# The prologue of a two-layer transformer kernel: when GpSimd splits a weight block, and in how many parts the modulation vectors are computed

## The chip, the cores and the metric

The kernel runs on one core of a Trainium2 chip. A core has five engines with instruction queues of their own, which meet only at semaphores: TensorE (PE, matmuls, with its weight loads shown as PEld), VectorE (DVE), ScalarE (ACT), GpSimd (POOL) and SyncE (SP, which here issues the DMAs). SBUF is the on-chip memory, PSUM the memory that TensorE writes. The metric is the time of one execution on the device in microseconds (us); the kernel before has a median of 677.3 us over three runs (677.08, 677.30 and 679.79).

## The reference

The input is x, 8 sequences of 256 tokens with 128 features. Two layers follow. Each has a modulation from a small conditioning input c: six vectors per layer, twelve in all, each for every sequence.

```python
mod = (_silu(L0_c) @ L0_wmod).reshape(8, 6, 1, -1)
sa, ca, ga, sb, cb, gb = (mod[:, i] for i in range(6))
ga = (2 * (ga >= 0) - 1) * jnp.maximum(jnp.abs(ga), 0.25)      # gb alike
h = _layernorm(x) * (1 + ca) + sa            # the first norm: needs sa and ca of layer 0 only
x = x + ga * attention(h)                    # 16 heads of 8, latent keys and values
h = _layernorm(x) * (1 + cb) + sb
x = x + gb * experts(h)                      # 8 experts, top 2, and a shared one
...                                          # layer 1, with its own six vectors:
x = x + ga * recurrent(_layernorm(x) * (1 + ca) + sa)   # gates, a scan over time, a gated MLP
x = x + gb * experts(_layernorm(x) * (1 + cb) + sb)     # 8 gated experts, top 2
```

In the attention, the latent is `gelu(h @ Wkd + bkd)`, its two halves added; keys and values come from it, and queries from h.

## The kernel before, in words

Tokens lie along the free dimension and features on the 128 partitions. The 2048 tokens are worked in four blocks of 512 (index t), a block being two sequences. The order on every engine is written out by hand in one function for each engine; what an engine may not start yet is held by a wait on a semaphore that stands in its queue, and everything behind that wait is held too.

The stages are: the prologue (loads, first norm, latent, values), the attention in 32 units (a sequence and a group of four heads each, n = 0 to 31), the first experts, the recurrent part of layer 1 with its MLP, and the second experts.

The prologue, engine by engine:

- **SP** loads the vectors, four blocks of x (L208), the modulation weights `WMOD` (L209, 768 KB), `KM`, and last the big block of matrices `M` (L211, 1384 KB), which holds also the recurrent layer's weights, 1664 columns of it.
- **TensorE** computes the means (L1140) of the four blocks, the variances of blocks 0 and 1 (L1153), then all twelve modulation vectors (L1190, 12 matmuls of 8 columns), then the variances of blocks 2 and 3, then the latent projection `kd` of the four blocks (L1199, waiting at L1198 for the two modulated sequences of its block). Then come the first unit's projections (L1207, L1208) and the values (L1314). A float32 matmul shows as two records in the profile.
- **ScalarE** squares (L386), takes logarithm and exponential of the variances (L392, L394), and later the four GELUs of the latent (L421), which wait for `kd`; a table load (L470) and the evacuation of unit 0 (L432 to L437) follow.
- **VectorE** centres (L645), waits for all twelve vectors, copies them out of PSUM (L767, L768), works out the gates (L771 to L779), and then normalises the four blocks: per block one multiplication by the reciprocal root (L652) and two `tensor_scalar` with the modulation (L656).
- **GpSimd** fills constants, flips signs in `KM` and `M` (L275 to L280), and then splits the recurrent layer's weights into an upper part `LH` (L282) and a rest `LL` (L284), each 128 x 1664. `LH` is also what TensorE's filler matmuls read (`keep_clock`, L1305). `LL` is first needed in layer 1, where TensorE waits for it at L1453. After the split GpSimd waits for the 32 `join` (L335), one for each attention unit.

In the attention, unit by unit, ScalarE evacuates a projection (L432 to L437), GpSimd joins it (L335), TensorE makes the scores (L1228, L1229), VectorE takes their maxima (L802) and spreads them into `MP` (`spread_max`: L813, then L815), TensorE transposes `MP` (`maxima_t`, L1282), VectorE adds it to the queries (L822), and TensorE makes the transposed scores (L1242 to L1246), whose exponentials ScalarE takes (L444); `values` (L1258, L1261), `spread_sum` (L828), `divide` (L836) and, once in four units, `place_values` (L843) complete it. GpSimd's own loop joins unit n + 3 at index n.

Of the kernel before, what the change touches and what calls it, by code (L numbers as in the profile page):

```python
# [5 lines left out]
BLK, NBLK = 512, 4  # L6
# [26 lines left out]
def build(nc, xT, wmod, vecs, mats, kmats, rows, b2, w0, w1, comb0, comb1, outT):  # L33
    f32, r32, bf16 = mybir.dt.float32, mybir.dt.float32r, mybir.dt.bfloat16
    ALU, ACT, AX = mybir.AluOpType, mybir.ActivationFunctionType, mybir.AxisListType
    ctx = ExitStack()
    with ctx:
        def sb(name, shape, dt=f32):
            return ctx.enter_context(nc.sbuf_tensor(name, shape, dt))

        def sem(name):
            return ctx.enter_context(nc.semaphore(name))

        def f(ap):
            return ap.bitcast(f32)

        def blk(tile, t, n=BLK):
            return tile[:, t * n:(t + 1) * n]
# [15 lines left out]
        LH = sb("LH", [128, MATS["l1"]], r32)  # L64
        LL = sb("LL", [128, MATS["l1"]], r32)
# [3 lines left out]
        MOD = sb("MOD", [128, 2, 6, 8])  # L69
        MC = sb("MC", [128, 2, 2, 8])  # L70
# [4 lines left out]
        SC = sb("SC", [128, 16])  # L75
# [7 lines left out]
        PS = ctx.enter_context(nc.psum_tensor("PS", [128, 8, 512], f32))  # L83
# [4 lines left out]
        def mat(name, i=0, n=128):  # L88
# [3 lines left out]
        WMOD = AR[:, 0:1536]  # L92
# [35 lines left out]
              for i, n in enumerate(("lg", "e", "k1", "k2", "e2", "w"))}  # L128
# [6 lines left out]
        const_done, ident_done, silu_done, mod_psum, mod_done, gate_done, sp_done = map(  # L135
            sem, ("const_done", "ident_done", "silu_done", "mod_psum", "mod_done", "gate_done", "sp_done"))
        mean_done, cen_done, sq_done, var_done, lnv_done, rstd_done, nrm_done, hn_done, hh_done, hl_done = map(
            sem, ("mean_done", "cen_done", "sq_done", "var_done", "lnv_done", "rstd_done", "nrm_done",
                  "hn_done", "hh_done", "hl_done"))
# [9 lines left out]
        l1_split = sem("l1_split")  # L149
        x_part = sem("x_part")  # L150
        qk_bias = sem("qk_bias")
        bias_done = sem("bias_done")
        flipped = sem("flipped")
        latent_one = sem("latent_one")
# [25 lines left out]
        def norm_at(k, t):  # L180

            return 8 + turns.index((k, t)) if k in (2, 3) else 4 * k + t
# [11 lines left out]
        def variance_bank(k, t):  # L194
            if k in (2, 3):
                return 4 + t
            return 6 + t % 2 if k == 4 else 4 + norm_at(k, t) % 2
# [51 lines left out]
        def _(gp):  # L249
# [29 lines left out]
            gp.tensor_scalar(qm[:, :, 0, :], qm[:, :, 0, :], -1.0, 0.0, ALU.mult, ALU.add).then_inc(flipped, 1)  # L279
            gp.tensor_scalar(qm[:, :, 2:4, :], qm[:, :, 2:4, :], -1.0, 0.0, ALU.mult, ALU.add).then_inc(flipped, 1)  # L280
            lm = M[:, MAT_AT["l1"]:MAT_AT["l1"] + MATS["l1"]]
            gp.tensor_scalar(LH[:, :], lm, 1.0, 0.0, ALU.mult, ALU.add).then_inc(l1_split, 1)  # L282
            gp.wait_ge(l1_split, 1)
            gp.tensor_tensor(out=LL[:, :], in0=lm, in1=f(LH[:, :]), op=ALU.subtract).then_inc(l1_split, 1)  # L284

            def split_weights(n, e, slot, width):

                s = moe[n]
                gp.tensor_scalar(WH[:, slot, 0:width], WS[:, 0:width], 1.0, 0.0, ALU.mult, ALU.add)\
                  .then_inc(s["split"], 1)  # L290
                gp.wait_ge(s["split"], 2 * e + 1)
                gp.tensor_tensor(out=WL[:, slot, 0:width], in0=WS[:, 0:width], in1=f(WH[:, slot, 0:width]),
                                 op=ALU.subtract).then_inc(s["split"], 1)
# [36 lines left out]
            def join(n):  # L330

                gp.wait_ge(qk_evac, 4 * n + 4)
                if n >= 4:
                    gp.wait_ge(st_done, 2 * n - 6)
                gp.tensor_tensor(out=QKX[:, n % 4, :, :], in0=QKT[:, :, :], in1=f(QKR), op=ALU.subtract)\  # L335
                  .then_inc(qx_ready, 2)
# [3 lines left out]
            for n in range(UNITS):  # L340
                if n + 3 < UNITS:
                    join(n + 3)
            gp.wait_ge(moe[0]["w_in"], 16)
            split_weights(0, 0, 0, 1024)
            for t in range(NBLK):
# [16 lines left out]
            for t in range(NBLK):  # L362
                for c in range(3):
                    i = 3 * t + c
# [277 lines left out]
        def _(dve):  # L642
# [2 lines left out]
                dve.tensor_tensor(out=blk(XC, t), in0=blk(X, t), in1=PS[:, mean_bank(k, t), :], op=ALU.subtract)\  # L645
                   .then_inc(cen_done, 1)

            def normalise(k, t):

                layer, which = k // 2 if k < 5 else 1, {0: 0, 1: 1, 2: 0, 5: 1}[k]  # L650
                dve.wait_ge(rstd_done, norm_at(k, t) + 1)
                dve.tensor_tensor(out=blk(HN, t), in0=blk(XC, t), in1=blk(STAT, t), op=ALU.mult)\  # L652
                   .then_inc(nrm_done, 1)
                dve.wait_ge(nrm_done, norm_at(k, t) + 1)
                for b in (2 * t, 2 * t + 1):
                    dve.tensor_scalar(blk(HN, b, SEQ), blk(HN, b, SEQ), MC[:, layer, which, b:b + 1],  # L656
                                      MOD[:, layer, 3 * which, b:b + 1], ALU.mult, ALU.add)\
                       .then_inc(hn_done, 1)

            def rms(k, src, weight, t):  # L660
                dve.wait_ge(rstd_done, norm_at(k, t) + 1)
                dve.scalar_tensor_tensor(out=blk(XC, t), in0=blk(src, t), scalar=vec(weight),
                                         in1=blk(STAT, t), op0=ALU.mult, op1=ALU.mult)\
                   .then_inc(nrm_done, 1)
# [97 lines left out]
                centre(0, t)  # L762


            dve.wait_ge(mod_psum, 1)
            mp = PS[:, 7, 0:96].rearrange("p (l i b) -> p l i b", l=2, i=6)
            dve.tensor_copy(MOD[:, :, :, :], mp).then_inc(mod_done, 1)  # L767
            dve.tensor_scalar(MC[:, :, :, :], mp[:, :, 1::3, :], 1.0, None, ALU.add).then_inc(mod_done, 1)  # L768
            dve.wait_ge(mod_done, 2)
            gates = MOD[:, :, 2::3, :]  # L770
            dve.tensor_scalar(GS[:, :, :, :], gates, 0.0, 2.0, ALU.is_ge, ALU.mult).then_inc(gate_done, 1)  # L771
            for layer in range(2):
                dve.scalar_tensor_tensor(out=GA[:, layer, :, :], in0=gates[:, layer, :, :], scalar=-1.0,
                                         in1=gates[:, layer, :, :], op0=ALU.mult, op1=ALU.max)\
# [5 lines left out]
                                     in0=GS[:, :, :, :].rearrange("p l w b -> p (l w b)"), scalar=-1.0,  # L780
                                     in1=GA[:, :, :, :].rearrange("p l w b -> p (l w b)"),
                                     op0=ALU.add, op1=ALU.mult).then_inc(gate_done, 1)
            for t in range(NBLK):
                normalise(0, t)
            def all_values(j):

                dve.wait_ge(v_psum, j + 1)
                dve.tensor_tensor(out=VALL[:, 4 * j:4 * j + 4, :],
                                  in0=PS[:, 2 + j, :].rearrange("p (i c) -> p i c", i=4),
                                  in1=ROWS[:, 0:128].unsqueeze(1).to_broadcast([128, 4, 128]), op=ALU.add)\  # L790
                   .then_inc(vall_done, 1)
# [113 lines left out]
            centre(1, 2)  # L905
            divide(31, 31, 0)
            normalise(1, 0)
            normalise(1, 1)
            attended(3)
            normalise(1, 2)  # L910
# [67 lines left out]
            for t in range(NBLK):  # L978
                i = projected.index((3, t))
# [3 lines left out]
                                         in1=blk(I_, t), op0=ALU.add, op1=ALU.mult).then_inc(hsi_done, 1)  # L983
# [140 lines left out]
        def _(pe):  # L1124
# [17 lines left out]
            def variance(k, t):  # L1142
                at = norm_at(k, t)
                pe.wait_ge(sq_done, at + 1)
                if k == 1 and t == 0:
                    pe.wait_ge(exp_done, 2 * UNITS)
                if k in (2, 3):
                    pe.wait_ge(cen_done, 8 + t + 1)
                    if k == 3:
                        pe.wait_ge(lnv_done, norm_at(2, t) + 1)  # L1150
                elif at >= 2:
                    pe.wait_ge(lnv_done, at - 1)
                pe.matmul(PS[:, variance_bank(k, t), :], OND[:, :], blk(STAT, t), start=True, stop=True)\  # L1153
                  .then_inc(var_done, 1)
# [30 lines left out]
            variance(0, 1)  # L1185
            pe.wait_ge(in_mod, 16)
            pe.wait_ge(silu_done, 1)
            for layer in range(2):
                for i in range(6):
                    mm = pe.matmul(PS[:, 7, 48 * layer + 8 * i:48 * layer + 8 * i + 8],  # L1190
                                   WMOD[:, 768 * layer + 128 * i:768 * layer + 128 * i + 128],
                                   SC[:, 8 * layer:8 * layer + 8], start=True, stop=True)
            mm.then_inc(mod_psum, 1)
            variance(0, 2)
            variance(0, 3)
            pe.wait_ge(in_mats, 16)
            for t in range(NBLK):
                pe.wait_ge(hn_done, 2 * t + 2)  # L1198
# [114 lines left out]
            for i in range(16):  # L1313
                mm = pe.matmul(PS[:, 2 + i // 4, 128 * (i % 4):128 * (i % 4) + 128],  # L1314
                               LAT[:, 128 * i:128 * i + 128], KM[:, 512:640], start=True, stop=True)
                if i % 4 == 3:
                    mm.then_inc(v_psum, 1)
            pe.wait_ge(ident_done, 9)
            pe.wait_ge(mod_done, 2)
            pe.wait_ge(l1_split, 1)  # L1320
            scores(0, 0, 0)
            project(1, 1, 0)
# [332 lines left out]
```

## Time and profile before

| | |
|---|---|
| median of three runs | 677.3 us |
| the profiled execution | 679.79 us, its span 678.0 us |
| PE, DVE, ACT, POOL busy | 606.8, 545.4, 486.1, 173.3 us |
| prologue, up to the end of the fourth `kd` matmul | about 29.1 us |
| one attention unit | about 4.4 us |

Times of the trace count from the start of the span; about 1.8 us of the execution lie outside it. "Busy" of PE counts a matmul from its start to a modelled end, so it says little about how full the array is. "PEclk" is the clock that TensorE was granted, 1.0 being 2.4 GHz and 0.50 being 1.2 GHz.

### The profile page before, as it was taken

What the parts mean: (1) busy time and instruction counts of PE and PEld (TensorE: products, weight loads), DVE (VectorE), ACT (ScalarE), POOL (GpSimd) and SP (SyncE); (2) the same over time, 40 slices, a digit from 0 to 9 for tenths busy, and PEclk for the clock granted to TensorE, in tenths of its full rate; (3) what the DMA queues carried; (4) which work ended last, traced back from release to release, by engine and by line L of the source; (5) the groups of instructions that cost most, each with busy time, mean ns of one, the idle gap of its engine ahead of it and who ended that gap; (6) DMA issues with size and microseconds to landing.
All of it is one profiled execution on the core that took longest, in us unless ns stands there. A gap on an engine that the chain in (4) does not pass through costs nothing.

```text
span 678.0 us, 11084 instructions
## 1 busy us (share of the span) xinstructions
PE 606.8 (89%) x3284; PEld 441.1 (65%) x3284; DVE 545.4 (80%) x1345; ACT 486.1 (72%) x857; POOL 173.3 (26%) x147
## 2 busy tenths in 40 slices
PE   8788889888997899999999999782699899999996
PEld 5355556555545568888888887351385788888884
DVE  3667888888866658878888887756899689999997
ACT  4548999999553669999999998677635466666663
POOL 3422223332301415443554443310143000000000
PEclk9789999999996899999999999976699799999999
DMA  7000000000100120122202220000000042222201
GB/s 239 1 0 2 2 2 0 0 0 0 32 1 0 48 113 37 57 95 94 91 2 93 93 85 1 23 1 0 0 1 0 1 150 87 87 86 86 86 1 62
DMA packets 6651, 29.85 MB, mean 44 GB/s; under 512 B 887, under 2 KB 1024, under 8 KB 4417
## 3 DMA queue, kind: packets, MB, share of 16 engines
q1 hardware_dynamic: 6610, 29.37, 12.2%
q8 instruction: 18, 0.29, 0.2%
q14 instruction: 23, 0.19, 0.1%
HBM read 28.18 MB, written 1.19 MB: 43 GB/s over the span
## 4 chain that ended last, share of the span: by engine, by line
PE 62%; DVE 26%; issue 5%; ACT 5%; DMA 1%; SPq 0%; POOL 0%; DVEq 0%; ACTq 0%; POOLq 0%
PE PS L1127 16%; PE PS L1129 16%; PE PS L1128 16%; DVE STAT L802 8%; PE PS L1273 2%; DVE RA L822 2%; PE PS L1228 2%; DVE HN L656 2%; PE PS L1153 2%; DMA AR<-in_wmod 1%; DVE SU L828 1%; PE PS L1242 1%; DVE HN L652 1%; ACT RA L605 1%; DVE AR L1086 1%
## 5 line engine op out<-in xcount | busy, mean ns | idle before, releaser
L937 DVE TENSOR_TENSOR RA<-AR,RA 128x512 fp32r<-128x512 f32 x140 | 134.3, 983 | 29.1 <-ACT RA L509 28.4
L508 ACT ACTIVATE AR<-PS,BI 128x512 f32<-128x512 f32 x144 | 99.4, 691 | 26.2 <-PE PS L1129 16.6
L1127 PE MATMUL PS<-HH,WH 128*128 128x512 f32 x272 | 109.5, 403 | 0.1
L1129 PE MATMUL PS<-HL,WH 128*128 128x512 f32 x272 | 107.4, 395 | 0.0
L1128 PE MATMUL PS<-HH,WL 128*128 128x512 f32 x272 | 107.3, 395 | 0.0
L509 ACT ACTIVATE RA<-PS,BI 128x512 fp32r<-128x512 f32 x144 | 98.4, 683 | 0.0
L802 DVE CUSTOM_DVE_ANT_0 STAT<-PS,MQ 128x128 f32<-128x128 f32 (+1 forms) x256 | 76.3, 354 | 20.2 <-PE PS L1229 20.1
L1127 PE MATMUL PS<-RA,WH 128*128 128x512 f32 x208 | 82.4, 396 | 2.5 <-DVE RA L1093 2.1
L1129 PE MATMUL PS<-RA,WH 128*128 128x512 f32 x208 | 81.2, 391 | 0.0
L1128 PE MATMUL PS<-RA,WL 128*128 128x512 f32 x208 | 81.2, 390 | 0.0
L312 POOL TENSOR_TENSOR AR<-AR 128x512 f32<-128x512 f32 x32 | 51.2, 1601 | 111.9 <-DVE AR L756 111.9
L335 POOL TENSOR_TENSOR RA<-QKT,RA 128x512 fp32r<-128x512 f32 x32 | 40.8, 1275 | 110.5 <-ACT RA L437 107.5
L605 ACT ACTIVATE RA<-AR 128x512 fp32r<-128x512 f32 x64 | 40.4, 632 | 34.2 <-DVE AR L1086 33.3
L1127 PEld LDWEIGHTS PS<-HH,WH 128*128 128x128 f32 x272 | 52.2, 192 | 15.6 <-ACT RA L509 3.0
L1129 PEld LDWEIGHTS PS<-HL,WH 128*128 128x128 f32 x272 | 51.9, 191 | 11.1
L1128 PEld LDWEIGHTS PS<-HH,WL 128*128 128x128 f32 x272 | 52.2, 192 | 10.7 <-issue 0.2
L444 ACT ACTIVATE AR<-PS 128x768 f32<-128x768 f32 x64 | 48.4, 808 | 13.7 <-PE PS L1246 11.6
L1153 PE MATMUL PS<-STAT,OND 128*128 128x512 f32 x48 | 31.5, 762 | 22.6 <-ACT STAT L386 22.6
L1093 DVE TENSOR_TENSOR RA<-AR,RA 128x512 fp32r<-128x512 f32 x64 | 44.3, 691 | 7.5 <-ACT RA L605 2.7
L599 ACT ACTIVATE AR<-PS 128x512 f32<-128x512 f32 x64 | 38.2, 597 | 13.8 <-PE PS L1129 11.8
L1127 PEld LDWEIGHTS PS<-RA,WH 128*128 128x128 f32 x208 | 39.2, 188 | 12.5 <-DVE RA L1093 3.2
L1086 DVE TENSOR_TENSOR AR<-AR 128x512 f32<-128x512 f32 x64 | 43.8, 685 | 2.2 <-ACT AR L614 2.2
(196 smaller groups left out, 1185.1 us busy)
## 6 DMA issues: line engine op xcount, KB each, us to landing
AR<-comb SPq DMA_DIRECT2D x16, 1024.0 KB, 4.6
WS<-in_w SPq DMA_DIRECT2D x9, 512.0 KB, 5.6
WS<-in_w SPq DMA_DIRECT2D x8, 384.0 KB, 3.1
M<-in_mats SPq DMA_DIRECT2D x1, 1384.0 KB, 12.2
X<-in_xT SPq DMA_DIRECT2D x4, 256.0 KB, 4.8
out_xT<-X SPq DMA_DIRECT2D x4, 256.0 KB, 2.1
AR<-in_wmod SPq DMA_DIRECT2D x1, 768.0 KB, 9.2
KM<-in_kmats SPq DMA_DIRECT2D x1, 162.5 KB
```

The costliest lines, as they stand in the source:

```text
L312: gp.tensor_tensor(out=blk(ACC, t), in0=blk(ACC, t), in1=YW[:, t % 2, :], op=ALU.add)\
L444: act.activation(PR[:, n0 % 2, 2 * h:2 * h + 2, :], PS[:, 2 + 2 * h:4 + 2 * h, 0:384], ACT.Exp, scale=SCALE).then_inc(exp_done, 1)
L508: act.activation(G[:, c, :], PS[:, c, :], ACT.Gelu_apprx_tanh, bias=bias).then_inc(s["act"], 1)
L509: act.activation(GH[:, m0 % 2, c, :], PS[:, c, :], ACT.Gelu_apprx_tanh, bias=bias)\
L605: act.activation(GH[:, m % 2, c, :], G[:, c, :], ACT.Copy).then_inc(s1["gh"], 1)
L802: mm = dve.tensor_tensor_reduce(out=MASKED_S[:, q, j, 0:width], in0=PS[:, j, first:first + width], in1=MQ[:, 256 - width:256], scale=-1.0, ...
L937: dve.tensor_tensor(out=GL[:, m0 % 2, c, :], in0=G[:, c, :], in1=f(GH[:, m0 % 2, c, :]), op=ALU.subtract).then_inc(s["lo"], 1)
L1086: dve.tensor_tensor(out=G[:, c, :], in0=G[:, c, :], in1=WB[:, e % 2, t * BLK:(t + 1) * BLK], op=ALU.mult).then_inc(s1["ymul"], 1)
L1127: pe.matmul(out, wh, xh, start=first, stop=False)
L1128: pe.matmul(out, wl, xh, start=False, stop=False)
L1129: return pe.matmul(out, wh, xl, start=False, stop=last)
L1153: pe.matmul(PS[:, variance_bank(k, t), :], OND[:, :], blk(STAT, t), start=True, stop=True)\
```

## The change

There are two edits.

The first is on GpSimd. `LH` is now made only once all eight sequences of the first norm are modulated (`hn_done` at 8), and `LL` not directly behind it but in the loop over attention units, at loop index 4, behind the join of unit 7.

The second is on TensorE and VectorE. The two vectors of the first norm are computed by two matmuls of their own (into PSUM bank 6), placed behind the variance of block 1. The twelve matmuls stay as they were but stand now behind the variances of blocks 2 and 3, ahead of `kd`. VectorE multiplies block 0 by its reciprocal root before it waits for the two vectors, copies only those, modulates, and copies the other ten and works out the gates after all four blocks.

```diff
@@ GpSimd
             lm = M[:, MAT_AT["l1"]:MAT_AT["l1"] + MATS["l1"]]
+            gp.wait_ge(hn_done, 8)
             gp.tensor_scalar(LH[:, :], lm, 1.0, 0.0, ALU.mult, ALU.add).then_inc(l1_split, 1)
-            gp.wait_ge(l1_split, 1)
-            gp.tensor_tensor(out=LL[:, :], in0=lm, in1=f(LH[:, :]), op=ALU.subtract).then_inc(l1_split, 1)
...
             for n in range(UNITS):
                 if n + 3 < UNITS:
                     join(n + 3)
+                if n == 4:
+                    gp.wait_ge(l1_split, 1)
+                    gp.tensor_tensor(out=LL[:, :], in0=lm, in1=f(LH[:, :]), op=ALU.subtract).then_inc(l1_split, 1)
@@ VectorE
+            divide_by_root(0, 0)
+            dve.wait_ge(mod_first, 1)
+            fp = PS[:, 6, 0:16].rearrange("p (i b) -> p i b", i=2)
+            dve.tensor_copy(MOD[:, 0, 0:2, :], fp).then_inc(mod_done, 1)
+            dve.tensor_scalar(MC[:, 0, 0, :], fp[:, 1, :], 1.0, None, ALU.add).then_inc(mod_done, 1)
+            dve.wait_ge(mod_done, 2)
+            modulate(0, 0)
+            for t in range(1, NBLK):
+                normalise(0, t)
             dve.wait_ge(mod_psum, 1)
...
-            dve.tensor_copy(MOD[:, :, :, :], mp).then_inc(mod_done, 1)
-            dve.tensor_scalar(MC[:, :, :, :], mp[:, :, 1::3, :], 1.0, None, ALU.add).then_inc(mod_done, 1)
-            dve.wait_ge(mod_done, 2)
+            dve.tensor_copy(MOD[:, 0, 2:6, :], mp[:, 0, 2:6, :]).then_inc(mod_done, 1)
+            dve.tensor_copy(MOD[:, 1, :, :], mp[:, 1, :, :]).then_inc(mod_done, 1)
+            dve.tensor_scalar(MC[:, 0, 1, :], mp[:, 0, 4, :], 1.0, None, ALU.add).then_inc(mod_done, 1)
+            dve.tensor_scalar(MC[:, 1, :, :], mp[:, 1, 1::3, :], 1.0, None, ALU.add).then_inc(mod_done, 1)
+            dve.wait_ge(mod_done, 6)
...
-            for t in range(NBLK):
-                normalise(0, t)
@@ TensorE
             variance(0, 1)
             pe.wait_ge(in_mod, 16)
             pe.wait_ge(silu_done, 1)
+            for i in range(2):
+                mm = pe.matmul(PS[:, 6, 8 * i:8 * i + 8], WMOD[:, 128 * i:128 * i + 128], SC[:, 0:8], start=True, stop=True)
+            mm.then_inc(mod_first, 1)
+            variance(0, 2)
+            variance(0, 3)
             for layer in range(2):
                 for i in range(6):
...
             mm.then_inc(mod_psum, 1)
-            variance(0, 2)
-            variance(0, 3)
             pe.wait_ge(in_mats, 16)
...
-            pe.wait_ge(mod_done, 2)
+            pe.wait_ge(mod_done, 6)
```

GpSimd's queue before, from the sign flips in `KM` and `M` on (`RA<-QKT,RA` is the join):

```order
L275 TENSOR_SCALAR KM<-KM 65x16x16
L276 TENSOR_SCALAR KM<-KM 65x16x8
L279 TENSOR_SCALAR M<-M 128x16x8
L280 TENSOR_SCALAR M<-M 128x16x16
L282 TENSOR_SCALAR LH<-M 128x1664
L284 TENSOR_TENSOR LL<-M,LH 128x1664
L335 TENSOR_TENSOR RA<-QKT,RA 128x512 x32
```

The same stretch of GpSimd's queue now:

```order
L276 TENSOR_SCALAR KM<-KM 65x16x16
L277 TENSOR_SCALAR KM<-KM 65x16x8
L280 TENSOR_SCALAR M<-M 128x16x8
L281 TENSOR_SCALAR M<-M 128x16x16
L284 TENSOR_SCALAR LH<-M 128x1664
L335 TENSOR_TENSOR RA<-QKT,RA 128x512 x8
L345 TENSOR_TENSOR LL<-M,LH 128x1664
L335 TENSOR_TENSOR RA<-QKT,RA 128x512 x24
```

The rest `LL` stands now between the eighth and the ninth join.

VectorE's queue before, from the centring on (`HN<-XC,STAT` is the multiplication by the root, `HN<-HN,MC,MOD` the modulation):

```order
L645 TENSOR_TENSOR XC<-X,PS 128x512 x4
L767 COPY MOD<-PS 128x96
L768 TENSOR_SCALAR MC<-PS 128x32
L771 TENSOR_SCALAR GS<-MOD 128x32
L773 SCALAR_TENSOR_TENSOR GA<-MOD 128x16 x2
L777 TENSOR_SCALAR GA<-GA 128x32
L779 SCALAR_TENSOR_TENSOR MG<-GS,GA 128x32
L652 TENSOR_TENSOR HN<-XC,STAT 128x512
L656 TENSOR_SCALAR HN<-HN,MC,MOD 128x256 x2
```

VectorE's queue now, from the same place:

```order
L648 TENSOR_TENSOR XC<-X,PS 128x512 x4
L654 TENSOR_TENSOR HN<-XC,STAT 128x512
L778 COPY MOD<-PS 128x16
L779 TENSOR_SCALAR MC<-PS 128x8
L662 TENSOR_SCALAR HN<-HN,MC,MOD 128x256 x2
```

The gates and the copies of the other ten vectors have moved behind the fourth block.

TensorE's queue before, from the means to the first unit's query projection (`PS<-SC,AR` are the modulation vectors, `64x512` is `kd`):

```order
L1140 MATMUL PS<-X,OND 128x512 x4
L1153 MATMUL PS<-STAT,OND 128x512 x2
L1190 MATMUL PS<-SC,AR 128x8 x12
L1153 MATMUL PS<-STAT,OND 128x512 x2
L1199 MATMUL PS<-HN,M 64x512 x4
L1207 MATMUL PS<-HN,M 128x256
```

TensorE's queue now, over the same stretch:

```order
L1159 MATMUL PS<-X,OND 128x512 x4
L1172 MATMUL PS<-STAT,OND 128x512 x2
L1208 MATMUL PS<-SC,AR 128x8 x2
L1172 MATMUL PS<-STAT,OND 128x512 x2
L1214 MATMUL PS<-SC,AR 128x8 x12
L1221 MATMUL PS<-HN,M 64x512 x4
L1229 MATMUL PS<-HN,M 128x256
```

The twelve small matmuls have changed places with the last two variances, and two more stand where the twelve stood.

## Rows read from the trace of the kernel before

**Rows 1.** The page: the chain that ended last, share of the span by engine.
```profile
PE 62%; DVE 26%; issue 5%; ACT 5%; DMA 1%; SPq 0%; POOL 0%; DVEq 0%; ACTq 0%; POOLq 0%
```

**Rows 2.** The chain in order of time, prologue: start, duration (us), what.
```profile
3.08 9.20 DMA AR<-in_wmod
...
12.32 2.86 PE PS L1190 x24
```

**Rows 3.** VectorE's instructions in order: start, duration (us), what, idle before.
```profile
16.30 0.69 DVE L652 TENSOR_TENSOR HN<-XC,STAT 128x512 f32<-128x512 f32 x1
17.02 2.22 DVE L656 TENSOR_SCALAR HN<-HN,MC,MOD 128x256 f32<-128x256 f32 x2
...
19.87 3.98 DVE L656 TENSOR_SCALAR HN<-HN,MC,MOD 128x256 f32<-128x256 f32 x2
...
24.50 0.73 DVE L656 TENSOR_SCALAR HN<-HN,MC,MOD 128x256 f32<-128x256 f32 x2
```

**Rows 4.** GpSimd's instructions in order, prologue.
```profile
17.48 1.61 POOL L282 TENSOR_SCALAR LH<-M 128x1664 fp32r<-128x1664 f32 x1
19.18 4.21 POOL L284 TENSOR_TENSOR LL<-M,LH 128x1664 fp32r<-128x1664 f32 x1
```

**Rows 5.** TensorE's instructions in order, prologue (two records to a matmul).
```profile
10.23 1.88 PE L1153 MATMUL PS<-STAT,OND 128*128 128x512 f32 x4
...
15.02 3.62 PE L1153 MATMUL PS<-STAT,OND 128*128 128x512 f32 x4
...
23.91 5.22 PE L1199 MATMUL PS<-HN,M 128*64 128x512 f32 x6 [3.48 <-DVE HN L656]
```

**Rows 6.** ScalarE's instructions in order, prologue.
```profile
12.01 0.63 ACT L394 ACTIVATE STAT<-STAT 128x512 f32<-128x512 f32 x1
...
14.30 0.61 ACT L386 ACTIVATE STAT<-XC 128x512 f32<-128x512 f32 x1
...
29.17 0.68 ACT L421 ACTIVATE AR<-PS,V 64x512 f32<-64x512 f32 x1 [0.86 <-PE PS L1199]
```

**Rows 7.** Windows: length, busy of PE, PEld, DVE, ACT, POOL, PEclk, DMA share, GB/s.
```profile
15.00:18.60 3.60, 3.60 (x6) 1.04 (x5) 3.25 (x10) 1.32 (x2) 2.25 (x3) 0.53 0.14 56
18.70:20.60 1.90, 1.04 (x2) 0.19 (x2) 1.86 (x3) 1.80 (x5) 1.82 (x2) 1.00 0.00 0
24.00:28.80 4.80, 4.80 (x6) 1.01 (x6) 3.02 (x10) 1.37 (x2) 0.00 (x0) 0.50 0.00 0
```

**Rows 8.** Weight loads of line 1153: duration in ns, least, median, most.
```profile
L1153 PEld LDWEIGHTS PS<-STAT,OND x8: 190/191/333, 9.8 to 16.7; 128*128 128x128 f32 x8
```

**Rows 9.** Lines 813 and 802: duration in ns, least, median, most.
```profile
L813 DVE CAST MP<-NM x32: 174/176/1042, 37.9 to 183.6; 128x8 fp32r<-128x8 f32 x32
...
L802 DVE CUSTOM_DVE_ANT_0 STAT<-PS,MQ x256: 282/356/425, 34.8 to 183.1; 128x128 f32<-128x128 f32 x64, 128x256 f32<-128x256 f32 x64
```

**Rows 10.** Units 0 and 6: GpSimd, VectorE and TensorE in order.
```profile
37.60 1.27 POOL L335 TENSOR_TENSOR RA<-QKT,RA 128x512 fp32r<-128x512 f32 x1 [3.45 <-ACT RA L437]
37.86 1.04 DVE L813 CAST MP<-NM 128x8 fp32r<-128x8 f32 x1
...
66.72 1.27 POOL L335 TENSOR_TENSOR RA<-QKT,RA 128x512 fp32r<-128x512 f32 x1 [3.21 <-ACT RA L437]
68.85 0.18 DVE L813 CAST MP<-NM 128x8 fp32r<-128x8 f32 x1
69.06 0.17 DVE L815 TENSOR_TENSOR MP<-NM,MP 128x8 f32<-128x8 f32 x1
69.34 0.38 PE L1282 MATMUL PS<-IDF,MP 128*128 128x128 f32 x2
...
71.33 1.27 POOL L335 TENSOR_TENSOR RA<-QKT,RA 128x512 fp32r<-128x512 f32 x1 [3.34 <-ACT RA L437]
```

**Rows 11.** TensorE by form, 39.0 to 42.4 us, then 42.5 to 46 us: busy us, mean ns.
```profile
L1228 PE MATMUL PS<-RA 32*128 32x128 f32 x2 | 0.5, 471 | 0.0
...
L1228 PE MATMUL PS<-RA 32*128 32x128 f32 x2 | 0.3, 322 | 0.1
```

More of the change, by code:

```diff
@@ L151, in build @@
         qk_bias = sem("qk_bias")
+        mod_first = sem("mod_first")
         bias_done = sem("bias_done")
@@ L646, in centre, with divide_by_root @@
                    .then_inc(cen_done, 1)
-            def normalise(k, t):
-                layer, which = k // 2 if k < 5 else 1, {0: 0, 1: 1, 2: 0, 5: 1}[k]
+            def divide_by_root(k, t):
                 dve.wait_ge(rstd_done, norm_at(k, t) + 1)
@@ L653, in normalise, with modulate @@
                    .then_inc(nrm_done, 1)
+            def modulate(k, t):
+                layer, which = k // 2 if k < 5 else 1, {0: 0, 1: 1, 2: 0, 5: 1}[k]
                 dve.wait_ge(nrm_done, norm_at(k, t) + 1)
@@ L658, in normalise @@
                        .then_inc(hn_done, 1)
+            def normalise(k, t):
+                divide_by_root(k, t)
+                modulate(k, t)
             def rms(k, src, weight, t):
```

## The prediction

> **What bounds the kernel now.** I read the page first: the chain that ended last is 62% TensorE and 26% VectorE, with 1% DMA and next to no GpSimd [rows 1]. GpSimd itself is thus not the bound. It can only matter by whom it holds up. The chain in order of time then shows who is late in the prologue: the modulation weights land 12.28 us into the span (3.08 + 9.20), the twelve small matmuls take 2.86 us behind them [rows 2], and only then does VectorE copy, work out the gates, and reach its first multiplication by the root at 16.30 [rows 3]. VectorE's instructions in order show the second thing. The two `tensor_scalar` of a block take 0.73 us where nothing disturbs them, but 2.22 us in block 0 and 3.98 us in block 1 [rows 3]. GpSimd's splits lie exactly there: `LH` from 17.48 to 19.09, `LL` from 19.18 to 23.39 [rows 4]. The excess is (2.22 - 0.73) + (3.98 - 0.73) = 4.74 us, and TensorE waits for it: 3.48 us of idle time before `kd` of block 1, which starts at 23.91 [rows 5]. The fourth `kd` ends near 29.13 (23.91 + 5.22), the last GELU starts at 29.17 [rows 5, 6], and all of unit 0 hangs on that one. So what the prologue gains is read at one point, the end of the fourth `kd`.
>
> The windows tell of TensorE's clock: it was granted 0.53 of full speed from 15.0 to 18.6, behind the twelve 8-column matmuls, 1.00 from 18.7 to 20.6, and 0.50 (1.2 GHz) from 24.0 to 28.8, behind a gap with one matmul in it [rows 7]. At 2.4 GHz two variances take 1.88 us, at the low clock 3.62, and three `kd` take 5.22 [rows 5]; so one such matmul is 0.94 us or 1.74 to 1.81 us.
>
> **The prologue after the change, step by step.** ScalarE has the root of block 0 at 12.64 (12.01 + 0.63) [rows 6]; VectorE multiplies until 13.3 (0.69 us) [rows 3]. The two first vectors are 4 of 24 records, 2.86 x 4/24 = 0.48 us, so they are there at 12.8 [rows 2]. Two small copies of about 0.2 us each and a pair of 0.73 us follow: block 0 is modulated at about 14.5. A square takes 0.61 us; that of block 2 stands right behind the root of block 0 and ends near 13.2, that of block 3 ended at 14.91 and can't come earlier [rows 6]. So TensorE, no longer held by twelve matmuls, does variance 2 at 13.2 and variance 3 from 14.93. Blocks 1 to 3 are then modulated at about 16, 18 and 19.6, at 0.69 + 0.73 us a block, with `LH` and `LL` out of the way. None of that is late, because TensorE has something else to do first: the twelve small matmuls now stand between variance 3 and `kd`. They were under the wait for the roots before; now they are on the path.
>
> - With the full clock throughout: 14.93 + 0.94 + 2.86 + 4 x 0.94 = 22.5. Gain 29.1 - 22.5 = 6.6 us.
> - With the low clock throughout: a weight load takes 0.33 us instead of 0.19 [rows 8], so the twelve take 2.86 x 0.33/0.19 = 5.0, and the sum is 14.93 + 1.81 + 5.0 + 4 x 1.74 = 28.7. Gain 0.4 us.
>
> What the clock does in between I can't know: small matmuls were followed by the low level before [rows 7], and two variances now lie among them. I take the middle, 3.5 us, and keep 0.4 and 6.6 as ends. The table load, the evacuation of unit 0, its join and its scores follow the last GELU as before and shift with it. The sign flips of `M`, as long as before, meet the modulation of block 2; TensorE's twelve matmuls hide that. `LH`, from about 19.6 to 21.3, is first needed at the scores of unit 0, behind the last `kd`, the GELU, a table load and the evacuation; it would have to be some 5 us late to be seen. The gates and the two additional copies, some 1.6 us on VectorE, fall in the same hole, even behind `LH`. SP issues nothing else, and no DMA is moved.
>
> **`LL` behind the join of unit 7.** GpSimd does nothing but one join of 1.27 us in each unit, and waits for 3.2 us in between [rows 10], so a piece of 4.21 us looks nearly free there. The join of unit 7 is the eighth, 66.72 to 67.99; `LL` would run from 68.09 to 72.30 by the times of before. Behind it in GpSimd's queue is the join of unit 8, which began at 71.33 [rows 10]. It would be 1 us late and end at 73.6; its first user, the scores of unit 8, stands behind a transposition one unit after the one at 69.34, so at 73.7 at the earliest: hidden. But VectorE has L813 at 68.85, a copy of 128 x 8 from SBUF to SBUF. It takes 176 ns in the median and once took 1042 [rows 9]. That once is unit 0: it started at 37.86 while GpSimd's join ran from 37.60 to 38.87, and it ended at 38.90, 0.03 us behind the join [rows 10]. So this copy waits for GpSimd's instruction to end, however small it is itself. Started at 68.85 under `LL`, it would end at 72.33 and not at 69.03: 3.3 us. Behind it in VectorE's queue are L815, the division, the sums' spreading, and the addition of the maxima; waiting for L815 is the transposition on TensorE, which started at 69.34 with 0.1 us to spare [rows 10]. The loss on the path is 3.2 us, and an attention unit has no slack that gives it back, as PE and DVE release each other in turn along the chain [rows 1]. Bounds: nothing, if the copy gets through, to 3.3.
>
> The Trainium skill, "SBUF — State Buffer", section "Who interferes with whom", speaks against the change at just this point: a copy in a mode that uses two ports and a GpSimd instruction exclude each other for a whole instruction, and whichever issues first goes first. The rows agree, 1042 ns under a join and 3.98 us under `LL`. If the two shared the port in proportion, as its page says they don't, the copy would lose a few tenths and the sum below would be 674.3.
>
> In these 3.2 us TensorE has nothing to do, and the last gap like it, 3.48 us, was followed by the low clock [rows 5, 7]. No row shows a whole unit at that clock; the nearest, the first scores' matmuls, take 471 ns instead of 322 [rows 11]. The low stretch between 15.0 and 18.6 lasted 3.4 us, from (1 - 0.53)/0.5 x 3.6 [rows 7]. 3.4 us of attention at that pace lose 3.4 x (1 - 322/471) = 1.1 us; two such stretches 2.2; none 0. It happens or not, so I take half of 1.1, that is 0.5.
>
> **The sum.** -3.5 + 3.2 + 0.5 = +0.2 us. On the profiled execution, 679.8 us with 678.0 us of span, that is 680.0. The profiled one was the slowest of the three; the median is 677.3, and the forecast for the median is 677.5 us. A difference of less than 0.5% (3.4 us) can't be told from no change in this kernel.
>
> **Rivals.**
>
> - *VectorE isn't held by `LL`.* Then only the prologue counts: 677.3 - 3.5 = 673.8, between 670.7 and 676.9 by the clock. For it: L802, which runs in every unit and beside the joins too, never took more than 425 ns, and only one L813 of 32 was ever long [rows 9]. Against it: that one waited to the end. 0.10.
> - *The clock holds through the prologue.* The two variances among the small matmuls keep TensorE at 2.4 GHz: -6.6 + 3.2 = 673.9. For it: after the first variances the clock was full. Against it: a single `kd` of 1.04 us ahead of a gap didn't hold it before [rows 7], and two with a dozen small ones might not either. 0.10.
> - *Slower: the low clock takes the prologue's gain and comes back in the attention.* The twelve small matmuls run at the low clock in front of `kd`, the fourth `kd` ends at 28.7, and the gap of 3.2 us in unit 6 is followed by one or two low stretches: -0.4 + 3.2 + 1.1 to 2.2 = +3.9 to +5.0, so 681.2 to 682.3. It decides once `kd` ends later than about 28. For it: three of four `kd` ran at 0.50 before [rows 7]. Against it: two variances in a row were followed by 1.00 at 18.7, and now TensorE's queue has no gap behind 15 us. 0.13.
> - *The two edits are too small to be seen for other reasons*, with some other wait of the same size ahead of unit 0: 677.3, 0.05.
>
> The forecast has 0.62. All of it, with its gain between 1.5 and 5.5 us, lies within 3.4 us of before, which gives 675.0 to 680.1 and counts as the same. Of the first two rivals about half passes the bound of faster (673.9): 0.11. Of the slower one nearly all passes 680.7: 0.12. Left for the same: 0.77. The range reaches from the middle of the first two rivals to the edge of the slower one, 673.9 to 681.0.
>
> **What would show it.** In the changed profile: all `tensor_scalar` of the modulation near 0.41 us each; the first multiplication at 12.7; the twelve small matmuls without a gap between variance 3 and the first `kd`; the last `kd` between 22.5 and 28.7, with PEclk saying why. In the attention: `LL` of 4.2 us behind the eighth join, one L813 (now with another line number) of 3.3 to 3.5 us under it, an idle TensorE ahead of one transposition, and perhaps a PEclk of 0.50 behind that. The prediction is wrong if that one copy is short, if something but `kd` sets the start of unit 0, or if the time moves by more than 3.4 us.

## The result, and the profile after

The changed kernel takes 736.17 us in the median of four executions (732.80 to 737.93), the kernel before 678.08 us (677.08 to 679.79). The ratio is 1.085, with a 95% interval of 1.081 to 1.088. I had forecast 677.5 us, 673.9 to 681.0, and the chance I gave to slower was 0.12.

The page of the changed kernel, part 2 (40 equal slices) and the chain's shares:

```profile
PE   8997999999999978999999999977369899999996
...
PEclk8798555555556968999999999998769889999999
...
PE 78%; DVE 13%; ACT 5%; issue 3%; DMA 1%; POOL 0%; SPq 0%; DVEq 0%; ACTq 0%; POOLq 0%
```

Eight slices in a row, of 18.3 us each, have a granted clock of about half (1.2 GHz). Before, the chain was 62% TensorE and 26% VectorE [rows 1]; now it is 78% and 13%. Something has made TensorE the bound of a whole stage.

First the prologue. TensorE's instructions in order, changed kernel (start, duration, what):

```profile
11.23 0.61 PE L1208 MATMUL PS<-SC,AR 128*128 128x8 f32 x4
12.28 1.13 PE L1172 MATMUL PS<-STAT,OND 128*128 128x512 f32 x2 [0.44 <-ACT STAT L389]
14.04 1.90 PE L1172 MATMUL PS<-STAT,OND 128*128 128x512 f32 x2 [0.63 <-ACT STAT L389]
15.73 5.13 PE L1214 MATMUL PS<-SC,AR 128*128 128x8 f32 x24
20.79 5.47 PE L1221 MATMUL PS<-HN,M 128*64 128x512 f32 x8
```

and two windows within `kd` (length, busy of PE, PEld, DVE, ACT, POOL, PEclk, DMA share, GB/s):

```profile
23.00:24.00 1.00, 1.00 (x2) 0.23 (x1) 0.00 (x0) 0.48 (x1) 0.00 (x0) 0.50 0.00 0
...
25.00:26.30 1.30, 1.30 (x4) 0.25 (x3) 0.00 (x0) 0.87 (x2) 0.00 (x0) 1.00 0.00 0
```

The fourth `kd` ends at 26.26 instead of 29.13 [rows 5]: 2.9 us earlier, where I had taken 3.5 between 0.4 and 6.6. About 0.9 us of that is not the change's: the blocks of x landed earlier in this execution, and the first variance began at 9.30, not 10.23. Counted from there the gain is 1.9 us. The twelve small matmuls run at the low clock (5.13 us, I had worked out 5.0), and `kd` stays at it until about 24.5 (the window from 24 to 25 us has 0.75); only its end is back at the high one. VectorE's modulation of a block takes 0.73 to 0.95 us, not 2.22 and 3.98 [rows 3].

Then unit 6 of the attention. GpSimd's instructions in order, then VectorE's, then TensorE's:

```profile
64.36 1.27 POOL L335 TENSOR_TENSOR RA<-QKT,RA 128x512 fp32r<-128x512 f32 x1 [3.21 <-issue]
65.59 3.70 POOL L345 TENSOR_TENSOR LL<-M,LH 128x1664 fp32r<-128x1664 f32 x1
69.25 1.26 POOL L335 TENSOR_TENSOR RA<-QKT,RA 128x512 fp32r<-128x512 f32 x1
```

```profile
66.48 2.84 DVE L832 CAST MP<-NM 128x8 fp32r<-128x8 f32 x1
69.36 1.18 DVE L834 TENSOR_TENSOR MP<-NM,MP 128x8 f32<-128x8 f32 x1
```

```profile
70.60 0.69 PE L1304 MATMUL PS<-IDF,MP 128*128 128x128 f32 x2 [3.46 <-DVE MP L834]
...
77.38 0.64 PE L1304 MATMUL PS<-IDF,MP 128*128 128x128 f32 x2
...
84.11 0.63 PE L1304 MATMUL PS<-IDF,MP 128*128 128x128 f32 x2
```

The stall is the one forecast, with one piece more: behind the copy, the subtraction of 128 x 8 (L834) also waits, until the join that follows `LL` is over at 70.51. Together they are about 3.7 us late, and TensorE is idle for 3.46 us. But then look at the distance of the transpositions, one to a unit: 6.78 and 6.73 us, where it was 4.39, from the 69.34 of [rows 10] to

```profile
73.73 0.39 PE L1282 MATMUL PS<-IDF,MP 128*128 128x128 f32 x2
```

The longer distance stays. Windows of the changed kernel (as above):

```profile
66.00:68.00 2.00, 1.14 (x6) 0.68 (x4) 1.97 (x5) 1.86 (x4) 2.00 (x1) 1.00 0.03 8
68.00:70.00 2.00, 0.00 (x0) 0.00 (x0) 1.97 (x2) 0.83 (x3) 2.00 (x2) 0.72 0.00 0
...
100.00:130.00 30.00, 30.00 (x194) 18.25 (x187) 17.86 (x105) 18.83 (x40) 5.96 (x5) 0.50 0.00 1
...
230.00:232.00 2.00, 2.00 (x6) 1.00 (x5) 1.97 (x3) 1.09 (x2) 2.00 (x1) 0.50 0.00 0
232.00:234.00 2.00, 2.00 (x5) 0.91 (x4) 0.95 (x5) 0.83 (x2) 0.02 (x1) 0.82 0.39 96
```

The clock falls to 1.2 GHz while TensorE waits, at about 68.9, and comes back at about 232.7 us, some 2.3 us into the first output projection, the first row of 128 x 512 matmuls since the stall:

```profile
230.39 4.76 PE L1295 MATMUL PS<-AR,M 128*128 128x512 f32 x8
```

For some 161 us of that TensorE is busy without a gap, and is the bound. At the low clock its attention matmuls are longer. One form, from 100 to 130 us, in the changed kernel (busy us, mean ns):

```profile
L1250 PE MATMUL PS<-RA 32*128 32x128 f32 x18 | 4.3, 472 | 0.0
```

and the same form in the same window of the kernel before:

```profile
L1228 PE MATMUL PS<-RA 32*128 32x128 f32 x28 | 4.6, 322 | 1.3 <-DVE NM L802 1.3
```

The account closes. The transposition of unit 6 is 1.26 us later than before (70.60 less 69.34: the stall of 3.6 less the 2.4 us by which its join was earlier, 64.36 for 66.72 [rows 10]). The last one, changed and before:

```profile
241.95 0.27 PE L1304 MATMUL PS<-IDF,MP 128*128 128x128 f32 x1
```

```profile
185.69 0.38 PE L1282 MATMUL PS<-IDF,MP 128*128 128x128 f32 x2
```

It is 56.3 us later. The span has grown by 733.7 - 678.0 = 55.7. So 55.0 us (56.3 - 1.3) lie between unit 6 and the last unit.

### The profile page after: what moved, and what is told of

Same layout as the page of the kernel before. It is cut to its first block, busy times and chain, and to the rows that moved or that the text cites. A ratio compares the mean times of both kernels' runs of the same rounds, so it can differ in the third digit from the quotient of the medians.

```text
span 733.7 us, 11097 instructions
## 1 busy us (share of the span) xinstructions
PE 676.5 (92%) x3288; PEld 479.8 (65%) x3288; DVE 548.8 (75%) x1349; ACT 490.6 (67%) x857; POOL 172.7 (24%) x147
## 2 busy tenths in 40 slices
DMA packets 6651, 29.85 MB, mean 41 GB/s; under 512 B 887, under 2 KB 1024, under 8 KB 4417
## 4 chain that ended last, share of the span: by engine, by line
PE 78%; DVE 13%; ACT 5%; issue 3%; DMA 1%; POOL 0%; SPq 0%; DVEq 0%; ACTq 0%; POOLq 0%
PE PS L1146 15%; PE PS L1148 15%; PE PS L1147 15%; PE PS L1268 4%; PE PS L1280 3%; PE PS L1250 3%; PE PS L1229 3%; PE PS L1230 3%; PE PS L1264 3%; PE PS L1295 2%; PE PS L1172 2%; PE PS L1304 2%; PE PS L1251 1%; PE PS L1283 1%; DVE STAT L821 1%
## 5 line engine op out<-in xcount | busy, mean ns | idle before, releaser
L447 ACT ACTIVATE AR<-PS 128x768 f32<-128x768 f32 x64 | 51.0, 810 | 37.6 <-PE PS L1268 37.6
L1095 DVE TENSOR_TENSOR AR<-PS,AR 128x512 f32<-128x512 f32 x64 | 43.9, 685 | 2.1 <-ACT AR L602 2.1
```

The source lines that it names most:

```text
L447: act.activation(PR[:, n0 % 2, 2 * h:2 * h + 2, :], PS[:, 2 + 2 * h:4 + 2 * h, 0:384], ACT.Exp, scale=SCALE).then_inc(exp_done, 1)
L1095: dve.tensor_tensor(out=G[:, c, :], in0=PS[:, 2 + c, :], in1=SG[:, c, :], op=ALU.mult)\
```

## The experiments

Theory A was: the stall lets the clock fall, and the attention's matmuls, which had kept the full clock before, don't bring it back. Against it stood B (the prologue's new order is to blame), C (`LL`'s place slows the attention by itself, by the port or by a shifted order), and later D (a gap is not enough, it takes GpSimd).

**`LL` in the prologue.**

```diff
             gp.wait_ge(hn_done, 8)
             gp.tensor_scalar(LH[:, :], lm, 1.0, 0.0, ALU.mult, ALU.add).then_inc(l1_split, 1)
+            gp.wait_ge(l1_split, 1)
+            gp.tensor_tensor(out=LL[:, :], in0=lm, in1=f(LH[:, :]), op=ALU.subtract).then_inc(l1_split, 1)
...
-                if n == 4:
-                    ...
```

> The changed kernel, with LL split directly behind the late LH, in the prologue, and no longer in the attention. Theory A (VectorE's copy is held by LL, TensorE stands still for 3.5 us, its clock falls to 1.2 GHz and the attention's matmuls never bring it back): no gap, so the clock stays at 1.00 through the attention and the time is before less the prologue's gain of 2.9 us, 675. Rival B (the new order of the prologue leaves the clock or the pipeline in a worse state for the attention): still about 730. Rival C (LL's place in the attention slows it by the shared port or by a shifted order, whatever the clock): 675 too.

676.39 us, ratio 0.998 (0.995 to 1.000). PEclk is 1.00 from 60 to 150 us. B falls: the prologue's order is that of the changed kernel.

**Only `LL` moved**, all else as before: the `LL` lines taken out of the prologue and put behind the join at loop index 4.

> The kernel before, with only LL moved behind the join of unit 7; LH and the whole prologue as before. Theory A: the gap and the low clock from unit 6 on, 678 + 4 + 25 units x 2.3 us = about 738. Rival B: only the stall, 682. Rival C: about 738.

733.62 us in two executions, ratio 1.083. The move of this one instruction costs 55.7 us of the 58.1 that both edits together cost. In its windows:

```profile
66.00:70.00 4.00, 0.94 (x6) 0.61 (x6) 3.88 (x6) 1.56 (x5) 2.97 (x2) 0.69 0.00 0
70.00:100.00 30.00, 30.00 (x198) 17.73 (x196) 17.62 (x102) 18.14 (x39) 5.10 (x4) 0.50 0.00 1
100.00:220.00 120.00, 120.00 (x751) 72.87 (x751) 70.70 (x402) 77.01 (x162) 22.52 (x18) 0.50 0.00 0
```

**The gap filled.** The changed kernel, `LL` where it is, and in unit 6 ahead of the transposition 14 fillers, matmuls of 128 x 512 whose results nobody reads (the diff is cut: TensorE's units 4 to 27 are also written out instead of looped):

```diff
+                if it == 0 and n0 == 5:
+                    pe.wait_ge(qm_ready, n + 1)
+                    pe.wait_ge(ot_done, n - 1)
+                    for _ in range(14):
+                        pe.matmul(PS[:, 7, :], LH[:, 0:128], LH[:, 0:512], start=True, stop=True)
...
```

> The changed kernel with LL where it is, but 14 filler matmuls (128 x 512, results unused) on TensorE ahead of the one transposition that waits for VectorE, so that TensorE has no gap. TensorE's step function for units 4 to 27 is written out instead of looped. Theory A: VectorE is still held for about 4 us, but the clock stays at 1.00: 678 - 2.9 + 4 = 679. Rivals B and C: still about 736.

679.95 us, ratio 1.004 (1.001 to 1.006). VectorE is held as long as before, TensorE has next to no gap. VectorE's instructions in order, TensorE's, then a window:

```profile
65.70 2.90 DVE L832 CAST MP<-NM 128x8 fp32r<-128x8 f32 x1
68.63 1.21 DVE L834 TENSOR_TENSOR MP<-NM,MP 128x8 f32<-128x8 f32 x1
```

```profile
66.02 3.54 PE L1321 MATMUL PS<-LH 128*128 128x512 f32 x14
69.90 0.44 PE L1304 MATMUL PS<-IDF,MP 128*128 128x128 f32 x2 [0.34 <-DVE MP L834]
```

```profile
75.00:150.00 75.00, 66.25 (x709) 44.08 (x708) 63.36 (x378) 68.56 (x153) 21.68 (x17) 1.00 0.01 2
```

C falls: `LL`, its lock, its late joins and the shifted order are all there, and 56 us of loss are gone with 14 fillers. (That the loop is written out is not what does it: it is so in the next run too, which has the low clock.) This run also prices the stall by itself: 679.95 against 676.39 with `LL` in the prologue, 3.6 us.

The kernel before holds a forerunner of this run, which I had overlooked. In unit 30 the subtraction of 128 x 8 was held 2.32 us by GpSimd's split of the experts' weights, while TensorE had an output projection to do. VectorE's line, GpSimd's, TensorE's:

```profile
175.86 2.32 DVE L815 TENSOR_TENSOR MP<-NM,MP 128x8 f32<-128x8 f32 x1
```

```profile
175.80 2.35 POOL L292 TENSOR_TENSOR WL<-WS,WH 128x1024 fp32r<-128x1024 f32 x1
```

```profile
175.29 3.60 PE L1273 MATMUL PS<-AR,M 128*128 128x512 f32 x8
178.73 0.38 PE L1282 MATMUL PS<-IDF,MP 128*128 128x128 f32 x2
```

TensorE has no gap ahead of that transposition, and the granted clock stays at 1.00 from 176 to 190 us.

**A burst later.** The changed kernel with 16 such fillers in unit 14.

> The changed kernel with 16 filler matmuls (128 x 512, results unused) in unit 14, long after the clock fell; TensorE's units 4 to 27 written out. Theory A: PEclk 0.50 from unit 6 to unit 14, then 1.00 to the end of the attention, about 679 + 9 x 2.3 + 5 for the fillers = 705. Theory A with a clock that doesn't hold after the burst: 736 + 5 = 741. Rivals B and C: 741.

704.68 us in two executions, ratio 1.040. Its windows:

```profile
100.00:125.00 25.00, 25.00 (x148) 15.29 (x150) 14.88 (x85) 15.88 (x33) 3.82 (x3) 0.50 0.00 1
...
130.00:135.00 5.00, 5.00 (x16) 3.94 (x15) 0.00 (x0) 2.29 (x6) 1.28 (x1) 0.64 0.00 0
135.00:140.00 5.00, 4.56 (x47) 3.01 (x45) 3.53 (x22) 1.90 (x3) 0.00 (x0) 1.00 0.00 0
140.00:180.00 40.00, 35.26 (x378) 23.47 (x376) 33.68 (x201) 36.51 (x81) 11.48 (x9) 1.00 0.01 2
```

The units on both sides of the burst hold the same instructions: at 0.50 before it, at 1.00 behind it, to the end of the attention. Sixteen dense matmuls, 5.85 us of them, buy back 31 us. So both clocks are levels at which this attention stays. What it is in its matmuls that doesn't raise the clock (shape, type or spacing) no run separates.

**Gaps without GpSimd.** `LL` in the prologue, and on VectorE ahead of the copy of unit 6 memsets of tiles that are free then:

```diff
                     maxima(n + 1, n0 + 1, 1)
+                    if n0 == 5:
+                        dve.memset(f(HL[:, 0:2048]), 0.0)
+                        dve.memset(XC[:, 0:2048], 0.0)
                     spread_max(n + 1, n0 + 1)
```

Two of 2048 columns:

> LL in the prologue as in the first experiment (676.4 us), and in the attention two memsets of 128 x 2048 on VectorE (1.76 us each in the prologue of before) ahead of the copy of unit 6, into tiles that are free then. They do nothing but hold TensorE's transposition for about 3.4 us, without GpSimd. Theory A (any gap of this length in the attention does it): PEclk 0.50 from unit 6 on, 676.4 + 3.4 + 25 x 2.3 = about 737. Rival D (it takes LL itself, its lock or GpSimd's late joins, to put the attention into its slow rhythm): 680.

736.65 us (two executions, as in the next two runs). 2048 and 1024 columns:

> As before it, but with memsets of 2048 and 1024 columns: a gap of about 2.5 us. Theory A with a fall at this length: about 736; without: 676.4 + 2.5 = 679. Rival D: 679. I lean to a fall, 6 to 4.

735.83 us. One of 2048:

> The same with one memset of 2048 columns: a gap of about 1.6 us. Theory A: short enough for the clock to stay, 676.4 + 1.6 = 678; if even this gap makes it fall, 735. Rival D: 678.

734.21 us. D falls. The transposition of unit 6 in the three, in this order:

```profile
70.40 0.69 PE L1306 MATMUL PS<-IDF,MP 128*128 128x128 f32 x2 [3.88 <-DVE MP L833]
```

```profile
71.12 0.69 PE L1306 MATMUL PS<-IDF,MP 128*128 128x128 f32 x2 [3.38 <-DVE MP L833]
```

```profile
69.42 0.44 PE L1305 MATMUL PS<-IDF,MP 128*128 128x128 f32 x2 [1.75 <-DVE MP L833]
```

An idle time of 1.75 us is enough. The windows of the last of the three, around and behind its gap:

```profile
68.00:69.00 1.00, 0.00 (x0) 0.00 (x0) 1.00 (x1) 1.00 (x4) 0.00 (x0) 1.00 0.00 0
...
70.00:71.00 1.00, 0.75 (x14) 0.46 (x15) 1.00 (x7) 0.83 (x2) 0.86 (x1) 1.00 0.00 0
71.00:72.00 1.00, 0.81 (x18) 0.54 (x12) 0.53 (x4) 0.38 (x1) 0.00 (x0) 0.66 0.00 0
72.00:73.00 1.00, 1.00 (x12) 0.47 (x8) 0.57 (x5) 0.05 (x1) 0.00 (x0) 0.50 0.00 0
```

The clock is full in the gap and behind it, and falls at about 71.3, while TensorE is working again. I had put 678 first for this run: wrong.

**Smaller gaps.** One memset of 1024 columns:

> LL in the prologue and one memset of 128 x 1024 ahead of the copy of unit 6: TensorE waits about 0.9 us longer than usual. A gap of 1.75 us brought the low clock. Theory A: 735 if this one does too, 677 if not; I lean to not, 6 to 4.

Its two executions took 731.13 us at a mean clock of 0.844, and 677.07 at 0.953. I had leaned to no fall. The profiled one is that of 731.13; its transposition waited 0.67 us at 68.37, and the clock fell at about 71.1. One of 256 columns:

> The same with a memset of 128 x 256: TensorE waits about 0.3 to 0.5 us longer than usual, as it does in every fourth unit behind the placing of the values. Theory A: the clock stays at 1.00, 676.5. If the added instruction and not the gap does it, 735.

677.28 us, ratio 0.999 (0.996 to 1.002), eight executions between 671.83 and 680.54. An added instruction does nothing by itself. But a small gap isn't tested by it: I had expected 0.3 to 0.5 us, and the transposition shows no wait at all:

```profile
67.67 0.44 PE L1305 MATMUL PS<-IDF,MP 128*128 128x128 f32 x2
```

And the 1024 columns once more:

> The kernel with one memset of 128 x 1024 once more, in many executions. Its first two took 731.13 and 677.07 us. Theory A (a gap of this length makes the clock fall or not, and once it has fallen the attention stays slow to its end): every execution is near 677 or near 731 to 736, none between, with a granted clock near 0.84 in the slow ones and 0.95 in the others. If the low clock could end by itself within the attention, times would be spread between the two.

732.44 us; all six executions lie between 727.77 and 735.32, at 0.839 to 0.849. The transposition waited 0.67 us in the profile:

```profile
71.69 0.44 PE L1305 MATMUL PS<-IDF,MP 128*128 128x128 f32 x2 [0.67 <-DVE MP L833]
```

Of eight executions of this kernel seven fell, by their times and mean clocks, and one did not, and none took a time in between. What decides in the one that did not isn't settled: the two traces are both of falling ones.

**`LL` in pieces.** Eight pieces behind eight joins (the diff is cut: the first piece waits for `LH`, and TensorE in layer 1 for all eight).

```diff
-                if n == 4:
-                    gp.wait_ge(l1_split, 1)
-                    gp.tensor_tensor(out=LL[:, :], in0=lm, in1=f(LH[:, :]), op=ALU.subtract).then_inc(l1_split, 1)
+                if 1 <= n <= 8:
+                    ...
+                    c = slice(208 * (n - 1), 208 * n)
+                    gp.tensor_tensor(out=LL[:, c], in0=lm[:, c], in1=f(LH[:, c]), op=ALU.subtract).then_inc(l1_split, 1)
```

> The changed kernel, with LL split in eight pieces of 208 columns, one behind each of the joins of units 4 to 11. A piece of about 0.5 us ends before VectorE's copy of the unit is due, 0.86 us behind the join. Theory A (GpSimd's work in the attention is harmless while no instruction of it lies under that copy): no gap, PEclk 1.00, 676, as with LL in the prologue. Rival C (GpSimd's additional work in the attention slows it whatever the clock): above 680.

675.98 us, ratio 0.997 (0.996 to 0.999): the lowest median, though not told apart from the 676.39 and 676.18 of `LL` in the prologue and of the run that follows. GpSimd's and VectorE's instructions in order, one unit of it:

```profile
47.34 1.27 POOL L335 TENSOR_TENSOR RA<-QKT,RA 128x512 fp32r<-128x512 f32 x1 [3.17 <-issue]
48.57 0.62 POOL L347 TENSOR_TENSOR LL<-M,LH 128x208 fp32r<-128x208 f32 x1
```

```profile
49.33 0.18 DVE L834 CAST MP<-NM 128x8 fp32r<-128x8 f32 x1
```

The piece ends at 49.19, the copy starts at 49.33 and takes its usual 0.18 us, and so it is in all eight units.

**The modulation edit alone**, with GpSimd's queue as before.

> The second edit alone: the two vectors of the first norm ahead of the other ten, with GpSimd's queue as before (LH and LL right behind the sign flips). Theory A: no gap in the attention, PEclk 1.00 there, so nothing near 735. The modulation of blocks 1 and 2 is again held by LH and LL until about 23, so the fourth kd ends at about 25 to 27 and the time is 675 to 678. Rival B (the new order of the prologue is the cause): 730 and more.

676.18 us, ratio 0.998 (0.995 to 1.000), PEclk 1.00 through the attention. VectorE's modulation pairs take 0.73, 2.21, 3.99 and 0.74 us, held again by the splits; still the fourth `kd` ends at 25.16, against 24.71 with `LL` behind the late `LH`. Counted from the start of the first variance, which takes the landing of x out, the fourth `kd` ends 18.9 us later before, 14.0 with only `LL` moved, 14.3 with only the modulation edit, 13.7 with both and `LL` behind the late `LH` (and 17.0 in the changed kernel's own profile, where the small matmuls had the low clock). So the two edits don't add: either brings nearly all of a gain of about 5 us.

These traces also show the small matmuls at the full clock. With `LL` behind the late `LH`:

```profile
16.70 2.74 PE L1213 MATMUL PS<-SC,AR 128*128 128x8 f32 x24
19.37 5.34 PE L1220 MATMUL PS<-HN,M 128*64 128x512 f32 x8
```

Of the twelve profiles that have TensorE's new order nine have them at 2.74 to 2.84 us, and three, the changed kernel's among them, at 5.13.

In the medians only 1.5 to 1.7 us are left of this, and only the pieces' interval excludes 1. Two things are on record for where the rest goes. The profiled execution of the kernel before is itself 1.7 us above its median. And with `LL` behind the late `LH` the 4.4 us at the fourth `kd` (29.13 less 24.71) are 1.9 us at the first transposition (39.49 for 41.37): between 34 and 38 us the granted clock was 0.50 there and 1.00 before, and the first eight fillers of the first unit took 3.97 us for 3.28. With the pieces, at a clock of 0.81 there, 6.2 us of 6.6 remain. The executions without a trace can't be split up so.

## Why the prediction was wrong, point by point

- *The prologue* was right in its order of work: the small matmuls are on the path, and the clock at which they run decides. That 2.9 us were found for the 3.5 forecast is in part luck. The middle of the two clocks is no state of its own: the gain, with the landing of x taken out, was 1.9 us where the small matmuls had the low clock and 5.2 where they had the full one (`LL` behind the late `LH`), inside the ends of 0.4 and 6.6.
- *The stall behind the join of unit 7* was right in place and cause: the copy of 128 x 8 waited 2.84 us for `LL`. Its size was 3.6 us for 3.2. The page that I drew on ("SBUF — State Buffer", the Trainium skill, "Who interferes with whom") also states that a VectorE instruction with two inputs in SBUF contends with a GpSimd instruction that reads SBUF. The trace agrees: L834, the subtraction, took 1.18 us under the following join instead of 0.17. I hadn't counted it, though the kernel before shows it in unit 30, 2.32 us; I had looked only at the copies.
- *The step that failed* is the one that priced the low clock in the attention, "3.4 us of attention at that pace lose 3.4 x (1 - 322/471) = 1.1 us; two such stretches 2.2". I took the length of a low stretch from the prologue, where 128 x 512 matmuls follow and end it. In the attention nothing ended it before the first output projection: most of 25 units at about 6.73 instead of 4.39 us. The term of 0.5 us, bounded at 2.2, was 55.0. The pace was right by its order (4.39 x 472/322 = 6.4, for 6.73); the duration, 3.4 us for some 163, was wrong by a factor of nearly fifty. Rows 7 themselves hold a longer stretch, 4.8 us at 0.50 with three `kd` in it, which I didn't use.
- *The rival with the clock held through the prologue* had its clock for the small matmuls in nine profiles of twelve, but not for `kd`, and its time of 673.9 still counted nothing for the attention.
- *The slower rival* had the right two elements, the gap and the low clock, and the same wrong length: 682.3 at the most. The criterion I gave it, a `kd` later than 28, had nothing to do with what decided.
- What the profile before held and I passed over: three groups of dense filler matmuls (L1305) stand in the first units, and the window from 40 to 42 us was at 0.50 in spite of the first eight. A stage that needs help to reach its clock should have made me ask what it does when it loses it.

## What to carry to other kernels

Ask of each stage not only what a fall of TensorE's clock costs while it lasts, but which later work would end it. A stage such as this attention can hold the full clock and yet not regain it, and then a stall of a microsecond is multiplied by the stage's whole length; fillers in the gap, or a burst behind it, are cheap against that. Here, work put in the idle time of GpSimd had to be cut to fit between VectorE's SBUF-to-SBUF copies, however small these are, since the copy waits for the end of the instruction and its reader waits for the copy.

## What the runs showed of the hardware that I had not expected

- The clock has two self-keeping levels under one and the same stream of attention instructions: 1.00 with 4.39 us a unit, 0.50 with 6.73 us a unit and TensorE without any gap for 161 us. Being always busy, as the profile counts it, did not raise it; 16 matmuls of 128 x 512 did, and so did the first output projection, 2.3 us after its start.
- In unit 6 an additional wait of TensorE of 0.67 us (as the two traces have it) made it fall in seven executions of eight, one of 1.75 us in both, and a memset of 0.27 us on VectorE, which left TensorE no wait, in none of eight. The duration from which on it falls isn't found.
- A fall can come after the gap: with the wait of 1.75 us it came about 2 us behind it, with that of 0.67 us 2.5 and 2.7 us behind it in the two traces, while matmuls were running.
